# One query projection per layer and batch, its row blocks made by ScalarE and VectorE

## The reference, cut to what matters

```python
x = x + xcond(layernorm(x), ctx, ctx, tau, delta, L0...)   # attention, layer 0
x = x + lora_ffn(layernorm(x), L0...)                      # dense FFN with a routed low-rank part
x = x + xcond(layernorm(x), ctx, ctx, tau, delta, L1...)   # attention, layer 1
x = x + moe(layernorm(x), L1...)                           # one of 8 experts for each row

def xcond(query, key, value, tau, delta, Wq, bq, ...):
    q = split_heads(query @ Wq.T + bq); k = split_heads(key @ Wk.T + bk); v = ...
    s = (einsum('bhqd,bhkd->bhqk', q, k) * tau + delta) / sqrt(8)
    return merge_heads(softmax(s) @ v) @ Wo.T + bo
```

## Time and profile before

| | us |
|---|---|
| median of three runs | 224.57 |
| the three runs | 222.85, 224.57, 227.26 |
| span of the profiled execution | 223.3 |
| TensorE busy in it | 180.6 |
| VectorE busy | 140.4 |
| ScalarE busy | 93.1 |
| GpSimd busy | 62.9 |

### The profile page before, as it was taken

One profiled execution on the slowest core, in us unless ns is written; L12 is line 12 of the kernel. 1 busy time (PEld: TensorE's weight loads), 2 busy tenths in 40 slices (PEclk: granted clock), 3 DMA queues, 4 the chain that ended last, 5 costly groups with the idle time before them and its releaser, 6 DMA issues.

```text
span 223.3 us, 3676 instructions
## 1 busy us (share of the span) xinstructions
PE 180.6 (81%) x1157; PEld 150.3 (67%) x1157; DVE 140.4 (63%) x385; ACT 93.1 (42%) x180; POOL 62.9 (28%) x68
## 2 busy tenths in 40 slices
PE   7676899979936997658999989985299949999970
PEld 2524776768825595337598669775199849999960
DVE  2889766767798236689725596554537436767760
ACT  2370354424810313423325534531286626777720
POOL 8793020000791002006001000005100744544562
PEclk9796799999995999999999999998555988999997
DMA  5899400000039100000000000001450272000000
GB/s 194 290 316 405 181 4 0 0 0 3 1 126 343 56 3 0 0 0 4 0 0 0 3 0 0 3 0 48 144 167 4 97 210 66 28 14 9 19 22 2
DMA packets 11983, 15.43 MB, mean 69 GB/s; under 512 B 1713, under 2 KB 8898, under 8 KB 11965
## 3 DMA queue, kind: packets, MB, share of 16 engines
q1 hardware_dynamic: 10444, 13.13, 17.7%
q0 software_dynamic: 1088, 1.60, 2.2%
q10 hardware_dynamic: 432, 0.47, 0.6%
HBM read 10.67 MB, written 5.44 MB: 72 GB/s over the span
## 4 chain that ended last, share of the span: by engine, by line
PE 42%; DVE 15%; issue 6%; ACT 4%; DMA 2%; POOL 2%; another core or an unknown queue 1%; DVEq 0%; ACTq 0%; POOLq 0%
PE scores L1011 8%; PE acc L1022 7%; PE acc L910 6%; PE shared L953 3%; PE shared L967 3%; PE shared L849 3%; DVE Ks L625 2%; PE scores L891 2%; PE shared L866 2%; PE shared L940 2%; DVE XN L603 2%; PE shared L821 1%; PE shared L1004 1%; DMA slots<-ROW,slot 1%; DVE stats L591 1%
## 5 line engine op out<-in xcount | busy, mean ns | idle before, releaser
L910 PE MATMUL acc<-VP,P 123*128 123x128 f32 (+1 forms) x320 | 42.9, 281 | 2.0 <-ACT P L534 2.0
L910 PEld LDWEIGHTS acc<-VP,P 123*128 123x128 f32 (+1 forms) x320 | 40.5, 195 | 5.2 <-ACT P L534 2.8
L534 ACT ACTIVATE P<-scores 123x512 f32<-123x512 f32 (+1 forms) x40 | 23.2, 595 | 36.5 <-PE scores L891 36.5
L460 POOL TENSOR_TENSOR X<-X,ROWS 128x512 f32<-128x512 f32 x6 | 8.1, 1352 | 86.2 <-DVE XN L603 86.1
L657 DVE TENSOR_REDUCE MR<-shared 128x4 f32<-128x308 f32 x64 | 27.1, 471 | 4.4 <-PE shared L866 3.8
L1011 PE MATMUL scores<-XST,HT 128*128 128x128 f32 x176 | 26.9, 303 | 3.4 <-ACT XST L564 3.4
L1011 PEld LDWEIGHTS scores<-XST,HT 128*128 128x128 f32 x176 | 24.7, 216 | 4.2 <-ACT XST L564 3.9
L474 POOL DMA_INDIRECT out<-XS,token x22 | 21.4, 974 | 20.1 <-DVE XS L789 17.2
L779 DVE TENSOR_TENSOR HT<-scores,B 128x512 f32<-128x512 f32 x22 | 15.2, 692 | 15.7 <-PE scores L1011 13.2
L1022 PE MATMUL acc<-W,HT 128*128 x176 | 24.9, 289 | 0.2 <-DVE XS L789 0.2
L866 PE MATMUL shared<-KG,QG 98*128 98x308 f32 x64 | 20.6, 384 | 5.1 <-DVE QG L648 4.0
(11 more groups left out here) (119 smaller groups left out, 271.6 us busy)
## 6 DMA issues: line engine op xcount, KB each, us to landing
W<-in_w SPq DMA_DIRECT2D x16, 256.0 KB, 8.0
slots<-XS SPq DMA_DIRECT2D x1, 2860.0 KB, 10.2
XS<-slots SPq DMA_DIRECT2D x2, 650.0 KB, 5.8
XS<-slots SPq DMA_DIRECT2D x2, 390.0 KB, 3.6
W<-in_ffn0w SPq DMA_DIRECT2D x1, 534.0 KB, 9.3
XS<-slots SPq DMA_DIRECT2D x2, 260.0 KB, 3.0
ATT<-in_att SPq DMA_DIRECT2D x1, 516.5 KB, 7.1
X<-in_x SPq DMA_DIRECT2D x2, 256.0 KB, 6.0
```

Source lines behind the costliest of these rows:

```text
L534: act.activation(P[0:w, n % NP], scores[n % 2][0:w, :], ACT.Exp).then_inc(probs_ready, 1)
L910: ins = pe.matmul(acc[qt // 2][:, c:c + VW], P[0:w, n % NP, 128 * qt:128 * qt + 128], VP[0:w, l, b, j, half], start=(t == 0 and qt % 2 == ...
```

## The change

The 96-column weights of the query are replaced by the plain 128 columns of `Wq`. One matmul per layer and batch (`q/l/b`) makes the projection of all four groups, group `g` in rows 32g to 32g + 31 of one bank. A new step `qs/l/b/g` makes the row blocks: ScalarE adds the bias and writes rows 0 to 31 of `QG`, waits for its own semaphore `qh_ready`, and copies rows 0 to 31 to rows 32 to 63; VectorE computes rows 64 to 95 from the bank and rows 0 to 31. The bank is free when all four groups have been through VectorE. The first `max` of a group waits for VectorE's step and for the copy. The weights of a layer shrink from 1033 to 777 columns. In the table, `q` and its four `qs` stand together, where the first `q` of the phase stood. In the diff the table is cut to the row of phase (0,1); line numbers of the changed kernel are 3 or 4 higher from ScalarE's part on (L521 becomes L522 and the new L525, L648 becomes L651, L849 L852, L866 L870, L875 L879, L891 L895, L910 L914).

```diff
--- before.py
+++ after.py
@@ -67,7 +67,7 @@
 RS8 = 1.0 / float(np.sqrt(np.float32(DK)))
 
 
-A_K, A_Q, A_V, A_O = 0, G * QR, 2 * G * QR, 2 * G * QR + D
+A_K, A_Q, A_V, A_O = 0, G * QR, G * QR + D, G * QR + 2 * D
 A_BK = A_O + D
 A_BQ = A_BK + G
 A_BV = A_BQ + G
@@ -104,23 +104,23 @@
...
-        xt/0/1 sc/0/0/2 max/0/0/12 sc/0/0/3 vp/0/1/1 q/0/1/0 max/0/0/13:15 pv/0/0/2:4 max/0/0/15 sc/0/0/4 mt/0/0/1
+        xt/0/1 sc/0/0/2 max/0/0/12 sc/0/0/3 vp/0/1/1 q/0/1 qs/0/1/0:4 max/0/0/13:15 pv/0/0/2:4 max/0/0/15 sc/0/0/4
...
@@ -290,6 +290,7 @@
         tau_ready = sem("tau_ready")
         v_ready = sem("v_ready")
         qh_ready = sem("qh_ready")
+        qc_ready = sem("qc_ready")
         ql_ready = sem("ql_ready")
         m_act = sem("m_act")
         m_dve = sem("m_dve")
@@ -350,7 +351,7 @@
             if kind == "kp":
                 return k_biased, G * key[1] + 2 * (key[2] + 1)
             if kind == "q":
-                return ql_ready, nth[key] + 1
+                return ql_ready, G * (nth[key] + 1)
             if kind == "mt":
                 return [(m_act, nth[key] + 1), (m_dve, nth[key] + 1)]
             if kind == "gate":
@@ -514,12 +515,14 @@
                         act.wait_ge(k_split, 1)
                     for b in range(B):
                         act.activation(Kt[:, :, b], Kf[:, :, b], ACT.Identity, scale=tau8[0:QR, b:b + 1]).then_inc(k_scaled, 1)
-                elif kind == "q":
+                elif kind == "qs":
                     _, l, b, g = s
-
-                    read(act, s)
-                    act.activation(QG[0:QR, b, g], bank(s)[0:QR, :], ACT.Identity,
-                                   bias=ATT[l][0:QR, A_BQ + g:A_BQ + g + 1]).then_inc(qh_ready, 1)
+                    read(act, ("q", l, b))
+                    r = slice(32 * g, 32 * g + 32)
+                    act.activation(QG[0:32, b, g], bank(("q", l, b))[r, :], ACT.Identity,
+                                   bias=ATT[l][r, A_BQ + g:A_BQ + g + 1]).then_inc(qh_ready, 1)
+                    act.wait_ge(qh_ready, nth[s] + 1)
+                    act.activation(QG[32:64, b, g], QG[0:32, b, g].bitcast(F32), ACT.Identity).then_inc(qc_ready, 1)
                 elif kind == "mt":
                     _, l, b, half = s
                     read(act, s)
@@ -641,12 +644,12 @@
                     v = bank(s)[0:w, 0:D].rearrange("p (s h c) -> p s h c", s=2, c=DK)
                     m = CON[0:w, C_VM + HALF * j:C_VM + HALF * (j + 1)].unsqueeze(1).unsqueeze(3).to_broadcast([w, 2, HALF, DK])
                     dve.tensor_tensor(o, v, m, ALU.mult).then_inc(v_ready, 1)
-                elif kind == "q":
+                elif kind == "qs":
                     _, l, b, g = s
-
+                    r = slice(32 * g, 32 * g + 32)
                     dve.wait_ge(qh_ready, nth[s] + 1)
-                    dve.scalar_tensor_tensor(QG[64:96, b, g], bank(s)[64:96, :], ATT[l][64:96, A_BQ + g:A_BQ + g + 1],
-                                             QG[64:96, b, g].bitcast(F32), ALU.add, ALU.subtract).then_inc(ql_ready, 1)
+                    dve.scalar_tensor_tensor(QG[64:96, b, g], bank(("q", l, b))[r, :], ATT[l][0:32, A_BQ + g:A_BQ + g + 1],
+                                             QG[0:32, b, g].bitcast(F32), ALU.add, ALU.subtract).then_inc(ql_ready, 1)
                 elif kind == "max":
                     _, l, b, i = s
                     n = (2 * l + b) * NQ * G + i
@@ -842,18 +845,19 @@
                     pe.matmul(bank(s)[0:w, 0:D], CTX[:, b, k0:k0 + w], ATT[l][:, A_V:A_V + D],
                               start=True, stop=True).then_inc(full[use[s][0]], 1)
                 elif kind == "q":
-                    _, l, b, g = s
+                    _, l, b = s
                     pe.wait_ge(in_att[l], 16)
                     pe.wait_ge(xnt_ready, nth["xt", 2 * l, b] + 1)
                     hold(s)
-                    pe.matmul(bank(s)[0:QR, :], ATT[l][:, A_Q + QR * g:A_Q + QR * (g + 1)], XNT[:, b], start=True,
+                    pe.matmul(bank(s)[:, :], ATT[l][:, A_Q:A_Q + D], XNT[:, b], start=True,
                               stop=True).then_inc(full[use[s][0]], 1)
                 elif kind == "max":
                     _, l, b, i = s
                     n = nth[s]
                     g, qt = divmod(i, NQ)
                     if qt == 0:
-                        pe.wait_ge(ql_ready, nth["q", l, b, g] + 1)
+                        pe.wait_ge(ql_ready, nth["qs", l, b, g] + 1)
+                        pe.wait_ge(qc_ready, nth["qs", l, b, g] + 1)
 
                         if (l, b) == (0, 0):
                             pe.wait_ge(kg_dve, min(g, 1) + 1)
@@ -1067,9 +1071,11 @@
         for g in range(G):
             for i in range(3):
                 rows_ = slice(32 * g, 32 * g + 32)
-                for c, cb, n in ((A_K, A_BK, "k"), (A_Q, A_BQ, "q")):
-                    out[:, c + QR * g + 32 * i:c + QR * g + 32 * (i + 1)] = a[p + "W" + n][rows_].T
-                    out[32 * i:32 * (i + 1), cb + g] = a[p + "b" + n][rows_]
+                out[:, A_K + QR * g + 32 * i:A_K + QR * g + 32 * (i + 1)] = a[p + "Wk"][rows_].T
+                out[32 * i:32 * (i + 1), A_BK + g] = a[p + "bk"][rows_]
+            for i in range(4):
+                out[32 * i:32 * (i + 1), A_BQ + g] = a[p + "bq"][rows_]
+        out[:, A_Q:A_Q + D] = a[p + "Wq"].T
         out[:, A_V:A_V + D] = a[p + "Wv"].T
         out[:, A_O:A_O + D] = a[p + "Wo"].T
         out[:, A_BV] = a[p + "bv"]
```

30 lines of the change are left out of this document (15 added, 15 removed).

## The result

| | before | after |
|---|---|---|
| median of four runs, us | 224.42 | 238.08 |
| the runs | 222.85 to 227.26 | 237.64 to 238.44 |
| span of the profiled execution | 223.3 | 236.5 |
| mean granted clock of TensorE in it | 0.908 | 0.869 |

The changed kernel is slower: ratio 1.0638, 95% interval 1.0578 to 1.0698. Ratios and intervals here leave out the runs of either kernel that lie over 1.5% above its fastest. The forecast of 231.7 us had the direction right; the loss is 13.7 us where it said 7.1, and 238.08 lies above its range, which ended at 236.5.

What follows compares the result with a forecast made beforehand. TensorE looked like the bound, but the chain of waits runs in short pieces over every engine. 223.3 us plus 4.3 for delays at four places, 3.5 for slow clock and 0.6 from span to median gave 231.7 us; range 226 to 236.5.

Steps and rivals of the forecast that it cites:

- (0,0): Phase (0,0): the key masking now stands behind all four low parts; +0.5 us, between 0 and 0.8.
- (0,1), block and clock: Phase (0,1): `mt` 3.6 us late, 3.0 of it come back, +0.7; slow TensorE clock after the empty stretch, +2.05.
- (1,0), block and clock: Phase (1,0): the last addition to X comes 1.1 us later; a slow TensorE clock adds 1.4.
- (1,1): Phase (1,1): exponentials, maxima and reductions wait for the block, scores start at 135.0 instead of 133.00; +2.0 us.
- What bounds the kernel: Whole kernel: TensorE looks like the bound, but waits are short pieces on every engine; query projection holds 6.5 us.
- The price of a group: ScalarE in each block: write 0.68 plus copy 0.63 less overlap 0.13, about 1.2 us; bounds 1.15 and 1.27.
- the third slow stretch: Rival: slow clock at (1,1) too, and long ones at the other places; 12.5 us, 236.4 us; chance 0.07.
- One slow stretch: Rival: the clock falls at (0,1), the longer gap, and holds at (1,0); 230.3 us; chance 0.20.
- the clock that holds: Rival: TensorE's clock does not fall at (0,1) or (1,0); 228.2 us; chance 0.18.
- The hidden stalls: Rival: copies run beside VectorE's work, period near 0.75, the 4.3 us shrink to about 0; 224.6 us; chance 0.10.
- Faster: Rival: the projections were the bound and leave the chain, 4.9 us off; 219.0 us; chance 0.05.
- Signs named in advance: Right: L522/L525 alternate at 1.2 us, clock 0.5 in 39-43 and 94-99 us; wrong: period under 1.0, new wait elsewhere.

Runs made afterwards that it cites:

- a_warm: Changed kernel plus 16, 14 and 10 filler matmuls where TensorE stood empty in the blocks of (0,1), (1,0) and (1,1): 228.38 us, ratio 1.0451.
- b_move: Kernel before with only q/1/0/3 moved out of the layernorm gap of (1,0), right behind q/1/0/2: 222.67 us, ratio 1.0207.
- a_warm_gap: Changed kernel with the three block fillings of `a_warm` and 10 more filler matmuls in the layernorm gap of (1,0): 227.36 us, 1.041 of before.
- a_nocopy: Changed kernel without ScalarE's copies to rows 32 to 63 of QG, which are set to zero once at the start: 228.31 us, ratio 1.0466.
- a_batch: Changed kernel with the four biased writes of a block first, then its four copies: 229.25 us, ratio 1.039.
- b_move_fill: `b_move` with 10 filler matmuls in the layernorm gap in place of the moved projection: 219.73 us, ratio 1.000.
- b_warm: Kernel before with 56 filler matmuls at seven places ahead of its own slow stretches, and 18 instead of 13 at the start: 217.56 us, ratio 0.9965.

## Why the prediction went wrong, step by step

| term | forecast, us | measured | from |
|---|---|---|---|
| (0,0) | +0.5 | 0 in one pair of executions | `XNT` of (0,0) and of (0,1) are both 1.65 late |
| (0,1), block and clock | 0.7 + 2.05 | 2.85, of it 1.3 clock | stretches after, `a_warm` |
| (1,0), block and clock | 1.1 + 1.4 | 2.99, of it 1.5 clock | the same |
| gap behind (1,0) | 0 | 2.40, all clock | `b_move`, `a_warm_gap` |
| (1,1) | 2.0 | 3.77, of it 1.2 clock | stretches after, `a_warm` |
| start, dense FFN, experts | 0 | +1.65, +0.67, -1.14 | stretches |
| sum of the spans | 7.8 | 13.2 | |
| from span to median | 0.6 | 1.6 | 236.5 and 238.08 |

The 0 of (0,0) is rough: from the first `XNT` to the second the kernel before took 21.50 and `b_move`, the same up to there, 19.39.

**What bounds the kernel** was right. TensorE is the busiest engine and twelve projections left it, but the end moved the other way, because at these places it waits for VectorE's reductions, and they for ScalarE.

**The price of a group** was mis-sized: 1.36 against 1.2, and over its upper bound of 1.27. The copy was right at 0.63. The overlap was wrong: it was read from two writes that stand behind each other in the earlier trace rows, where it is 0.10 by their own durations (0.67 each), and carried over to a pair in which one waits for the other. Block ends came out at T + 5.46 on ScalarE and T + 5.57 on VectorE, against 4.9 and 5.1. That is half a microsecond at each place. Exponential 8 starts 5.46 after its block's begin, not 4.9, and the second `mt` of (0,0) 6.95 after the first write of (0,1), not 6.5.

**Phase (0,1)** came out right in its shape (reductions late, three projections less, the `pv` behind at half speed). That its sum of 2.75 meets 2.85 is luck: the block cost 1.55 with the clock held, not 0.7, with reductions late by 4.1 and not 3.6, and the clock 1.3, not 2.05.

**Phase (1,0)** had the mechanism and lacked half a microsecond: the block cost 1.53 and not 1.1, the longer period; the clock's 1.4 was right.

**The step that failed** is the sentence "The fourth projection of before lay in a gap of TensorE and gives nothing back." It gives nothing back, but it was taken for worthless from that. This work in a gap had no price in time and still had an effect: with it the clock stayed granted. In before the clock is 1.00 all through 97 to 118 us; in after it is 0.50 from 96.2 to 116.7; `a_warm` shows that it falls in the gap with the block filled too, and `b_move` that the move of this one projection is enough. The cost is 2.40 us, and without it the time would be near 235.7, inside the range. The prediction applied the clock where its own sums made a new gap, and did not ask where an old gap had lost its filling.

**Phase (1,1)**: the third slow stretch was a rival with a chance of 0.07, and it occurred. TensorE stood idle there for 2.52 us ahead of the fourth `max`, against 4.53 and 3.36 at the other two places, and about as long as the 2.60 of the earlier trace rows, behind which the clock had still been 1.00. Here it was 0.50 from 140.8. The length of one gap was no ground to give this place so small a chance. The clock's 1.2, which the sum did not have, and the block's 2.53 instead of 2.0 make the 1.8 over the forecast.

**The rivals.** One slow stretch and the clock that holds are excluded, since the clock fell at three blocks. The hidden stalls are excluded, since the period was 1.36 and not near 0.75. Faster is excluded by the time. The third stretch came true in its mechanism, and its 236.4 was nearest. The nearness is in part luck: it had 7.9 us of clock, where the blocks had 4.0 and the gap 2.4, and its base of 4.6 is not the 4.3 of the sum, nor is it worked out. Two other numbers do not follow from what is said of them: the hidden stalls give 223.9 and not 224.6, and the lower end of the range 227.0 and not 226. Of the result's distance to the forecast, 6.4 us, the gap has 2.4, phase (1,1) 1.8, (1,0) 0.5, start, dense FFN and experts 1.2 in balance, (0,1) 0.1, (0,0) -0.5, and the step from span to median 1.0.

**Signs named in advance.** The alternation of L522 and L525 (at 1.36, not 1.2), the low parts with reductions right behind them, and a clock of 0.5 in both stretches named (from 41.6 and from 96.2 us) are there. So is the last one on the list of what would make the prediction wrong, a cost outside the four places: the gap behind (1,0).

**The range** ended at 236.5, since its upper end came from cases that each had the clock at known places. The measure of the second chip (232.78 us against 218.4) is a ratio of 1.070, so the miss does not hang on one chip.

## What to carry to other kernels

When a change takes an instruction out of an engine's idle time, ask what that instruction did for the work behind it: a matmul in a gap can cost nothing and keep the clock. Before a chain of small steps is bundled into one block, look at what stands behind the block in each in-order stream; it is late by the whole block, also where the total of work shrinks. Then look at the order inside the block: here the writes first and the copies after them took 1.8 us off the wait behind it. Price a row of dependent instructions by its full durations, and take an overlap only from a row of the same pair.

## What the runs showed of the hardware

- Four ScalarE writes from one PSUM bank stand 0.70 apart with 0.68 each (2.79 for four in `a_nocopy`), so there is no overlap. Four copies from SBUF to SBUF start 0.52 apart (2.19 for four in `a_batch`) with 0.61 to 0.63 each, an overlap of 0.09. The Trainium skill, page "ScalarE: Activation LUTs", section "What ACT_TABLE_LOAD costs", gives 93 ns for the overlap of instructions that follow each other; the copies agree, the writes don't. Two writes of the kernel before, from two banks, did overlap, by 0.10. The shared bank alone does not explain it: in `a_nocopy` the exponential behind the fourth write reads another bank and starts 0.02 after the write's end (35.72). Nor does VectorE's reading: in `a_batch` the second write starts 0.03 after the first one's end and 0.01 before VectorE reads the bank. What decides it is open.
- Ten matmuls of 128 columns ahead of the transposes held the clock at 1.00 over a gap in which and behind which it fell to 0.50 without them (`b_move_fill` and `b_move`). In one of two executions with 14 matmuls in the block of (1,0) it fell all the same (`a_warm_gap`).
- A memset of GpSimd on one tile stretches VectorE's four instructions on another from 1.12 to 2.65 us when they meet. They took 2.37 to 2.84 in the three executions in which they met and 1.11 to 1.12 in the other eleven. The Trainium skill, page "SBUF — State Buffer", section "Who interferes with whom", tells of a port pair that the two share; the rows agree in direction.
- With three shared PSUM banks and the fourth for the projections alone the kernel before is 9% slower (`b_three`), and the projections wait 15.1 us for their own bank.
- In `b_warm` a higher mean clock (0.95 to 0.98 instead of 0.91 to 0.93 on that chip) was worth 0.35%, within the interval of no change.
